# The keys' convolution as three products of split operands with 128 moving columns

## The reference

```python
q, k, v = h @ wq.T, h @ wk.T, h @ wv.T                 # 64 heads of 8 channels
dw = conv(qkv, dw_kernel, 5x5, one kernel a channel)   # depthwise
pw = conv(dw, pw_kernel, 1x1, groups of 8 channels)
qkv_all = concatenate([qkv, pw])                       # plain heads and convolved heads
query, key_, value = relu(f[:8]), relu(f[8:16]), f[16:24]   # of each group of 24
scores = einsum('bhdn,bhen->bhde', value_pad, key_)
out = einsum('bhde,bhen->bhdn', scores, query)         # divided by its last row
y = conv(out, proj_kernel, 1x1) * bn + shift + x
```

## Time and profile before

| | us |
|---|---|
| median of 3 runs (lowest, highest) | 5199.48 (5190.54, 5200.01) |
| profiled execution | 5196.7 |
| its span, first to last instruction | 5194.8 |
| PE busy in the span | 4887.5 |
| DVE, ACT, POOL busy | 2583.4, 2021.1, 1223.1 |

### The profile page before, as it was taken

One profiled execution on the slowest core, in us unless ns is written; L12 is line 12 of the kernel. 1 busy time (PEld: TensorE's weight loads), 2 busy tenths in 40 slices (PEclk: granted clock), 3 DMA queues, 4 the chain that ended last, 5 costly groups with the idle time before them and its releaser, 6 DMA issues. The chain is left out here.

```text
span 5194.8 us, 65292 instructions
## 1 busy us (share of the span) xinstructions
PE 4887.5 (94%) x22760; PEld 3445.3 (66%) x22760; DVE 2583.4 (50%) x3635; ACT 2021.1 (39%) x3671; POOL 1223.1 (24%) x1030
## 2 busy tenths in 40 slices
PE   8999999999999999999999996899899989998958
PEld 7887887888888888888888883344344434443423
DVE  3333333333334334424434421786688578847865
ACT  3333333333333333333323320454555455545555
POOL 2342342342342332332332330000300020011003
PEclk9999999999999999999999998999999999999969
DMA  6666665666666666666656644443344344434313
GB/s 188 198 208 202 197 214 199 198 212 205 198 216 202 204 206 206 206 197 215 206 186 225 203 151 168 142 155 112 130 136 150 108 144 130 141 118 135 117 35 115
DMA packets 390811, 893.09 MB, mean 172 GB/s; under 512 B 33488, under 2 KB 66512, under 8 KB 388240
## 3 DMA queue, kind: packets, MB, share of 16 engines
q1 hardware_dynamic: 390544, 889.18, 51.8%
HBM read 588.74 MB, written 300.32 MB: 171 GB/s over the span
## 5 line engine op out<-in xcount | busy, mean ns | idle before, releaser
L733 POOL TENSOR_TENSOR toeplitz<-taps 128x512 f32<-128x512 f32 x768 | 889.1, 1185 | 955.2 <-PE bank L441 955.2
L441 PEld LDWEIGHTS bank<-toeplitz,columns 128*128 128x128 f32 x8192 | 954.4, 192 | 13.9
L441 PE MATMUL bank<-toeplitz,columns 128*128 128x128 f32 x8192 | 955.7, 275 | 0.0
L1029 PE MATMUL bank<-att,w_proj 128*128 128x512 f32 x2048 | 909.6, 598 | 34.1 <-DVE centred L1314 23.8
L1029 PEld LDWEIGHTS bank<-att,w_proj 128*128 128x128 f32 x2048 | 393.0, 192 | 531.8 <-issue 523.3
L356 PE MATMUL bank<-x_hi,w_hi 128*128 128x512 f32 x1536 | 610.9, 398 | 18.4 <-DVE x_lo L600 18.4
L1362 POOL TENSOR_TENSOR centred<-centred,x_out 128x512 f32<-128x512 f32 x128 | 164.5, 1318 | 1937.1 <-ACT centred L1176 1937.1
L358 PE MATMUL bank<-x_lo,w_hi 128*128 128x512 f32 x1536 | 601.2, 391 | 0.0
L357 PE MATMUL bank<-x_hi,w_lo 128*128 128x512 f32 x1536 | 599.7, 390 | 0.0
L1042 PE MATMUL bank<-edge,w_branch 128*128 128x512 f32 x1024 | 494.5, 629 | 96.1 <-ACT edge L1130 96.1
L671 DVE TENSOR_SCALAR ckey_t<-bank 128x256 f32<-128x256 f32 x256 | 107.4, 419 | 881.8 <-PE bank L441 881.4
(11 more groups left out here) (115 smaller groups left out, 5629.8 us busy)
## 6 DMA issues: line engine op xcount, KB each, us to landing
x_sb<-in_x_tiled SPq DMA_DIRECT2D x128, 1024.0 KB, 6.4
tiles_dram<-tiles SPq DMA_DIRECT2D x128, 867.0 KB, 6.8
loaded<-tiles_dram SPq DMA_DIRECT2D x256, 433.5 KB, 4.0
inverse<-inverse_dram SPq DMA_DIRECT2D x256, 256.0 KB, 5.0
att_dram<-out_sb SPq DMA_DIRECT2D x256, 256.0 KB, 4.1
att<-att_dram SPq DMA_DIRECT2D x64, 1024.0 KB, 6.3
xb<-x_dram SPq DMA_DIRECT2D x128, 330.0 KB, 3.2
x_out<-in_x_pad SPq DMA_DIRECT2D x32, 1056.0 KB, 5.5
```

Source lines behind the costliest of these rows:

```text
L441: last = nc.tensor.matmul(bank[:, v * M:(v + 1) * M], columns[:, h % 2, t - T_K, v + b, a * HT:(a + TO) * HT], w[:, t, d, :], start=(d == ...
L733: last = nc.gpsimd.tensor_tensor(toeplitz[:, h % 2, t, :].rearrange("p (d o r) -> p d o r", o=HD, r=PL), tap, point, ALU.mult)
L1029: last = nc.tensor.matmul(P_BANKS[m][:, :], w_proj[:, i * HALF + k, m * P:(m + 1) * P], att[:, i, k, :], start=(i == 0 and k == 0), stop=( ...
```

## The change

For k the columns and the matrix are split as x is in the plain stage. ScalarE copies k's blocks with rounding into `columns_hi` (one buffer, `round_k`) and k's taps into `tk_hi` (one buffer, `round_taps`); VectorE subtracts into `columns_lo` and, in place of `toeplitz`, `tk_lo` (`split_k`, `split_taps`). TensorE adds three products for each block and shift, 24 a head with 128 moving columns each. v stays as it is; its gather is three copies of 136 elements. The taps of head 0 are rounded and split in the plain stage (chunks 5 and 6). SP's `load_head` waits for `k_split` too. `score_d` shrinks to one row of 240 columns, of which the denominators use shifted windows, so one VectorE write a half is left out; `score_n` shares its room with `score_t`.

```diff
+        columns_lo = ctx.enter_context(nc.sbuf_tensor("columns_lo", [P, 2, 2, HV + 1, TG * HT], F32R))
+        columns_hi = ctx.enter_context(nc.sbuf_tensor("columns_hi", [P, HV + 1, TG * HT], F32R))
+        tk_lo = ctx.enter_context(nc.sbuf_tensor("tk_lo", [P, 2, 3, len(SHIFTS) * M], F32R))
+        tk_hi = ctx.enter_context(nc.sbuf_tensor("tk_hi", [P, len(SHIFTS) * M], F32R))
-        score_d = sb("score_d", [P, NCH * P])
+        score_d = sb("score_d", [P, 2 * P - SH])
...
                             sp.wait_ge(columns_ready, SH * it + h + 1)
+                            sp.wait_ge(k_split, SH * it + h + 1)
                             load_head(h + LR)
...
-                        last = nc.tensor.matmul(DEN_BANK[:, :], score_d[:, j * P:(j + 1) * P], rows((relu_q, relu_c)[half], j),
+                        last = nc.tensor.matmul(DEN_BANK[:, :], score_d[:, P - SH * (j + 1):2 * P - SH * (j + 1)], rows((relu_q, relu_c)[half], j),
...
+                    pe.wait_ge(k_split, SH * it + h + 1)
+                    pe.wait_ge(tk_split, SH * it + h + 1)
+                    if h >= 2:
+                        pe.wait_ge(cevac[T_K], SH * it + h - 1)
+                    for v in range(HV):
+                        for d, (a, b) in enumerate(SHIFTS):
+                            to, reach = k_bank[:, v * M:(v + 1) * M], slice(a * HT, (a + TO) * HT)
+                            high, low = columns_hi[:, v + b, reach], columns_lo[:, h % 2, 0, v + b, reach]
+                            wide, narrow = tk_hi[:, d * M:(d + 1) * M], tk_lo[:, h % 2, T_K, d * M:(d + 1) * M]
+                            nc.tensor.matmul(to, high, wide, start=(d == 0), stop=False)
+                            nc.tensor.matmul(to, high, narrow, start=False, stop=False)
+                            last = nc.tensor.matmul(to, low, wide, start=False, stop=(d == len(SHIFTS) - 1))
+                    last.then_inc(cready[T_K], 1)
...
+                        if j == 5:
+                            act.wait_ge(head_done, SH * it)
+                            round_taps(it, 0)
                         key(it, j)
...
                     for v in range(HV + 1):
-                        last = copy(columns[:, h % 2, :, v, :].rearrange("p t (a v) -> p t a v", v=HT),
-                                    loaded[:, h % LR, T_K:, :].rearrange("p t (a c) -> p t a c", c=TG)[:, :, :, v:v + TO - 1:HV])
+                        last = copy(columns[:, h % 2, T_V - T_K, v, :].rearrange("p (a v) -> p a v", v=HT),
+                                    loaded[:, h % LR, T_V, :].rearrange("p (a c) -> p a c", c=TG)[:, :, v:v + TO - 1:HV])
                     last.then_inc(columns_ready, 1)
 
+                def round_k(it, h):
+                    act.wait_ge(tiles_loaded[h % LR], 16 * (SH // LR) * it + 16 * (h // LR) + 16)
+                    if h >= 1:
+                        act.wait_ge(cready[T_K], SH * it + h)
+                    for v in range(HV + 1):
+                        last = copy(columns_hi[:, v, :].rearrange("p (a v) -> p a v", v=HT),
+                                    loaded[:, h % LR, T_K, :].rearrange("p (a c) -> p a c", c=TG)[:, :, v:v + TO - 1:HV])
+                    last.then_inc(k_rounded, 1)
+
+                def round_taps(it, h):
+                    act.wait_ge(tk_built, SH * it + h + 1)
+                    copy(tk_hi[:, :], toeplitz[:, h % 2, T_K, :]).then_inc(tk_rounded, 1)
+
                 def conv(it, last):
+                    round_k(it, 0)
                     gather(it, 0)
...
+                        if h + 1 < SH:
+                            round_k(it, h + 1)
+                            round_taps(it, h + 1)
...
-                    nc.vector.tensor_scalar(score_d[:, 0:last].rearrange("p (j s) -> p j s", s=apart)[:, :, 0:SH],
-                                            mask[:, None, :].to_broadcast([P, NCH - 1, SH]), key_sum[:, 0:1], None, ALU.mult)
-                    nc.vector.tensor_scalar(score_d[:, last:last + SH], mask[:, :], key_sum[:, 0:1], None,
+                    nc.vector.tensor_scalar(score_d[:, P - SH:P], mask[:, :], key_sum[:, 0:1], None,
                                             ALU.mult).then_inc(sums_placed, 1)
...
+                def split_k(it, h):
+                    dve.wait_ge(k_rounded, SH * it + h + 1)
+                    for v in range(HV + 1):
+                        last = nc.vector.tensor_tensor(
+                            columns_lo[:, h % 2, 0, v, :].rearrange("p (a v) -> p a v", v=HT),
+                            loaded[:, h % LR, T_K, :].rearrange("p (a c) -> p a c", c=TG)[:, :, v:v + TO - 1:HV],
+                            columns_hi[:, v, :].bitcast(F32).rearrange("p (a v) -> p a v", v=HT), ALU.subtract)
+                    last.then_inc(k_split, 1)
+
+                def split_taps(it, h):
+                    dve.wait_ge(tk_rounded, SH * it + h + 1)
+                    nc.vector.tensor_tensor(tk_lo[:, h % 2, T_K, :], toeplitz[:, h % 2, T_K, :], tk_hi[:, :].bitcast(F32),
+                                            ALU.subtract).then_inc(tk_split, 1)
...
+                        if j == 6:
+                            split_taps(it, 0)
                     keys_by_position(it, NCH - 2)
                     keys_by_position(it, NCH - 1)
                     mask_scores(it, 0)
+                    split_k(it, 0)
                     invert(it, 0)
...
                             ALU.max).then_inc(cevac[T_K], 1)
+                        if h + 1 < SH:
+                            split_k(it, h + 1)
+                            split_taps(it, h + 1)
                         if 4 <= h < NCH + 4:
                             divide(it, 0, h - 4)
```

More of the change, by code:

```diff
@@ L84, in attention @@
         loaded = sb("loaded", [P, LR, 3, TN])
-        columns = sb("columns", [P, 2, 2, HV + 1, TG * HT])
-        toeplitz = sb("toeplitz", [P, 2, 3, len(SHIFTS) * M])
+        with nc.sbuf_tensor("columns", [P, 2, 2, HV + 1, TG * HT], F32) as columns:
+            pass
+        columns_lo = ctx.enter_context(nc.sbuf_tensor("columns_lo", [P, 2, 2, HV + 1, TG * HT], F32R))
+        columns_hi = ctx.enter_context(nc.sbuf_tensor("columns_hi", [P, HV + 1, TG * HT], F32R))
+        with nc.sbuf_tensor("toeplitz", [P, 2, 3, len(SHIFTS) * M], F32) as toeplitz:
+            pass
+        tk_lo = ctx.enter_context(nc.sbuf_tensor("tk_lo", [P, 2, 3, len(SHIFTS) * M], F32R))
+        tk_hi = ctx.enter_context(nc.sbuf_tensor("tk_hi", [P, len(SHIFTS) * M], F32R))
         q_stage = sb("q_stage", [M, 2, TT])
-        score_n = sb("score_n", [P, P])
-        score_d = sb("score_d", [P, NCH * P])
+        with nc.sbuf_tensor("score_n", [P, P], F32) as score_n:
+            pass
         score_t = sb("score_t", [P, P])
+        score_d = sb("score_d", [P, 2 * P - SH])
         w_proj = sb("w_proj_part", [P, C])
@@ L143, in attention @@
         toeplitz_ready = sem("toeplitz_ready")
+        tk_built = sem("toeplitz_k_built")
+        tk_rounded = sem("toeplitz_k_rounded")
+        tk_split = sem("toeplitz_k_split")
+        k_rounded = sem("k_columns_rounded")
+        k_split = sem("k_columns_split")
         cready = [sem(f"conv_{n}_ready") for n in "qk"]
@@ L433, in conv_head @@
                     last.then_inc(cready[T_Q], 1)
-                    pe.wait_ge(columns_ready, SH * it + h + 1)
[L436 to L444, removed]
+                    pe.wait_ge(k_split, SH * it + h + 1)
@@ new lines, in conv_head @@
+                    last.then_inc(cready[T_K], 1)
+                    pe.wait_ge(columns_ready, SH * it + h + 1)
+                    if h >= 2:
+                        pe.wait_ge(cevac[T_V], SH * it + h - 1)
+                    for v in range(HV):
+                        for d, (a, b) in enumerate(SHIFTS):
+                            last = nc.tensor.matmul(v_bank[:, v * M:(v + 1) * M],
+                                                    columns[:, h % 2, T_V - T_K, v + b, a * HT:(a + TO) * HT],
+                                                    w[:, T_V, d, :], start=(d == 0), stop=(d == len(SHIFTS) - 1))
@@ L446, in conv @@
+                    last.then_inc(head_done, 1)
                 def conv(it):
@@ L587, in mask_scores @@
                     dve.wait_ge(den_evac, START + 2 * it + half)
-                    apart, last = P + SH, (NCH - 1) * (P + SH)
-                    nc.vector.tensor_scalar(score_d[:, 0:last].rearrange("p (j s) -> p j s", s=apart)[:, :, 0:SH],
-                                            mask[:, None, :].to_broadcast([P, NCH - 1, SH]), key_sum[:, 0:1], None, ALU.mult)
-                    nc.vector.tensor_scalar(score_d[:, last:last + SH], mask[:, :], key_sum[:, 0:1], None,
+                    nc.vector.tensor_scalar(score_d[:, P - SH:P], mask[:, :], key_sum[:, 0:1], None,
                                             ALU.mult).then_inc(sums_placed, 1)
@@ L734, in build @@
```

(2 more changed lines are left out.)

## The result

| | us |
|---|---|
| before, median of 4 runs | 5199.74 |
| after, median of 4 runs (5500.8 to 5511.18) | 5503.23 |
| ratio, 95% interval | 1.0593 (1.0578 to 1.0608) |
| forecast | 5438 (5400 to 6145) |

The kernel is 5.9% slower. 5438 was 65 us short; the sign, the case (load-bound) and the range held. The range is wide, for it had to take in the four-pass case.

A forecast was written before the change was run, and what follows sets the result against it. The forecast took TensorE to bound the attention layer's conv stages. Added weight loads +228.6, late heads +13 and score_d -3 made +239 on 5196.7, 5435; the runs' median lies 2.8 higher, so 5438 us, range 5400 to 6145.

The forecast's parts named there:

- load-bound: Short fp32r matmuls for k each cost one weight load, 111.6 ns, giving 5438 us; chance 0.53.
- four-pass case: k's fp32r matmuls take four passes a column, 216 to 229 ns each, 6066 to 6145 us; chance 0.27.
- TensorE, +228.6 us: k in each conv-stage head: 24 loads at 111.6 ns for 16, +0.893 us a head over 256 heads.
- load and stream in turn: At 128 columns a load doesn't run under the matmul before it: 165 ns each, 5752 us; chance 0.08.
- some 80 ns: In between for k's matmuls, as in the skill's section on the gap: 5240 us, slower by 0.8%; chance 0.05.
- the stream's 69 ns: If loads don't bound k's matmuls, the stream does: 69 ns each, 5161 to 5186 us; faster or equal, chance 0.07.
- The 15 ns over: Time beyond one pass a column on each fp32r matmul, seen at 512 columns; 92 us more at the range's top.
- The chain, hidden: ScalarE's and VectorE's rounding and splits between k(h) and k(h+1): 2.7 us under 3.52 of cover, 0.8 left, no cost.
- The late head, +13 us (0 to 25): Head 9, 15 iterations: VectorE, delayed by the next weights' split, about 0.9 us late for k: +13 us.
- The forecast's own range, 5405 to 5540: The load-bound case's range: from loads at 110 ns and no late head to 15 ns over on each matmul.
- score_d, -3 us: Write for seven chunks left out before the denominators: 0.2 us saved, 16 times.

The follow-up runs named there:

- e4: The changed kernel with the weights' split after head 12, each of k's 24 matmuls moving 64 columns, not 128: 5421.16 us.
- e3: The changed kernel with the weights' split after head 12 and k's third product left out, 16 matmuls a head for 24: 5249.44 us.
- e6: The kernel before with only the weights' split moved from head 7 to head 12: 5187.83 us, ratio 0.9987.
- e2: The changed kernel with GpSimd's build for head h waiting until VectorE has split k's columns of head h - 1: 5414.43 us, ratio 1.0428.

## Why the prediction was right, and where it fell short

- **TensorE, +228.6 us.** Right by mechanism and size. One fp32r matmul of 128 columns costs one load, 112 ns; e4 shows that 64 or 128 columns make no difference, e3 that 16 of them cost what 16 f32 instructions cost, and the 64-column loads behind e4 that the floor goes with the stationary columns. The four passes (216 ns, 0.27), load and stream in turn (165 ns, 0.08), some 80 ns (0.05) and the stream's 69 ns (0.07) are ruled out by the 112 ns themselves. The 15 ns over that widened the range upward didn't appear while the load bounds. The 81 ns of the Trainium skill's page "TensorE: Matmul & The Clock Gate", section "Back-to-back issue gap", isn't what this chip does with fp32r operands; the measured 112 decides.
- **The chain, hidden.** Right: 1.0 us spare where 0.8 was forecast. The copies and subtractions took 0.78 and 0.72 us for three, not 0.9.
- **The late head, +13 us (0 to 25).** This is the step that failed, in size: the place, the head and the mechanism's first half were named, but it measured 83. Counted from k(7) through (about 1229.8) in the stage shown, forecast and measured: division ends 4.3 and 5.0; weights 8.6 and 8.4; k(8)'s bank 9.0 and 8.7; split_k(9) 9.9 and 11.6; split_taps(9) 10.6 and 12.2. The forecast priced split_k at its length with no build beside it, though the late VectorE meets the next build; its row was that of `score_n`, which reads one operand from TensorE's bank, where split_k reads both from SBUF, the on-chip memory. The sign was on record: the weights' subtraction took 2.49 us in the earlier trace rows and takes 1.76 in the kernel after, where almost no build runs beside it. And the forecast gave the standing still no second price: in 13 of 15 iterations the clock fell after it, worth 2.9 us a time on average, more than the wait itself.
- **The forecast's own range, 5405 to 5540.** 5503 lies in it by luck. Its top left 92 us for 15 ns over on each matmul, which didn't come, and the late heads used that room. (Loads at 110 ns and no late head give 5415 by the forecast's terms, not 5405.)
- **score_d, -3 us.** Not measured alone; the denominators' wait in the stage shown fell from 0.98 to 0.79 us, and most plain stages are 0.2 us shorter, as forecast.
- **The rest.** 5435 on the profiled execution, plus 70 for the late heads, is 5505; it took 5500.8. Between them lie the first heads (+2), the plain stages beyond the 3 us of score_d (-5) and the edge layer.

## What to carry to other kernels

Count weight loads before column passes: where each matmul brings its own load of 112 ns, three split products pay only if their columns make up for it. With f32 at two instructions a product, as here, three fp32r ones gained at 256 columns (3 x 124 = 372 ns for 2 x 216 = 432) and lost at 128 (3 x 112 = 336 for 2 x 112 = 224). And when a new wait is "just late", price what the late engine will meet in its new place, and what TensorE's clock does after a stop; moving one unrelated job, the weights' split, by five heads was worth 89 us.

## What the runs showed of the hardware that was not expected

- A VectorE subtraction with both operands in SBUF, 296 ns at the median for 136 elements, took up to 1146 ns, about as long as one of GpSimd's own instructions there (1.10 us), in the heads where it ran beside GpSimd's multiplication, and at most 330 ns once GpSimd was ordered behind it. The division (L680) went from 812 to 1269 ns on average, with 600 to 660 ns where no build runs beside it and up to 1497 where one does: in the kernel after most of them run beside one. It can go the other way too: in e6 the weights' subtraction had started 0.5 us ahead of the build and kept its 1.76 us, and the build's first instruction took 2.16 us, where the average is 1.185. By the Trainium skill, page "GPSIMD Engine Reference", section "Specifications", GpSimd shares its SBUF interfaces with VectorE and they contend where VectorE's instruction has two SBUF inputs; these runs agree.
- 2.45 us of standing still on TensorE were followed by some 3.5 to ten microseconds at a granted clock of 0.50 in 13 of 15 iterations, in a stretch with TensorE busy throughout, and by none in two. Stops of 1.81 us (e3) were followed by it in 9 of 14 iterations, waits of 0.20 us (e2) in none. What decides it in a given iteration is not shown.
